# Splitting the softmax denominators of the last three batches over three engines, and moving the last pair's denominators ahead of its values

## What is computed

```
scores = einsum('bnhl,bkl->bhnk', CqWqk, C_kv) / sqrt(32)
attn = softmax(scores, axis=-1)
V_up = (C_kv @ Wv_u).reshape(b, nkv, H, HD)
out = einsum('bhnk,bkhd->bnhd', attn, V_up)
```

## Time and profile before

| | us |
|---|---|
| median of 3 runs | 678.75 (678.68 to 680.32) |
| the profiled execution | 681.57 |
| its span, first to last instruction | 679.6 |
| PE busy | 591.6 (87%) |
| POOL busy | 424.9 (63%) |
| DVE busy | 442.2 (65%) |
| ACT busy | 303.8 (45%) |

### The profile page before, as it was taken

How to read it: one execution, slowest core, us unless ns; L and a number is a source line. 1 busy time by engine, 2 the same in 40 slices (tenths; PEclk the granted TensorE clock), 3 DMA queues, 4 the chain that set the end, 5 groups by cost and what they waited for, 6 DMA issues and landing times.

```text
span 679.6 us, 12918 instructions
## 1 busy us (share of the span) xinstructions
PE 591.6 (87%) x3856; PEld 306.8 (45%) x3856; DVE 442.2 (65%) x717; ACT 303.8 (45%) x641; POOL 424.9 (63%) x394
## 2 busy tenths in 40 slices
PE   4863988699999999998999999999999899986965
PEld 4331644353544554464456354455446444433322
DVE  2711796378776887489658867588758966745451
ACT  1330144335644374346534564337444744563450
POOL 5002027558965886598776896488659877789300
PEclk9895889799999999999989999999999999997896
DMA  8567630353116510481018311661048101100000
GB/s 310 211 210 245 236 119 18 78 210 166 43 29 228 211 44 1 115 323 57 17 42 271 154 43 31 225 215 43 1 130 333 32 15 47 43 9 1 22 1 14
DMA packets 31410, 77.22 MB, mean 114 GB/s; under 512 B 11378, under 2 KB 25042, under 8 KB 28915
## 3 DMA queue, kind: packets, MB, share of 16 engines
q1 hardware_dynamic: 31186, 75.36, 33.1%
q10 hardware_dynamic: 160, 1.05, 0.4%
HBM read 58.66 MB, written 2.88 MB: 91 GB/s over the span
## 4 chain that ended last, share of the span: by engine, by line
PE 62%; DVE 12%; issue 7%; POOL 6%; ACT 5%; SPq 3%; DMA 3%; POOLq 0%; ACTq 0%; DVEq 0%
PE st_ps L649 11%; PE mx_ps L677 10%; PE pv_ps L664 9%; POOL acc L1096 5%; PE mi_ps L459 4%; PE mi_ps L466 4%; PE mi_ps L453 4%; PE mi_ps L512 4%; SPq L371 3%; PE mi_ps L631 2%; DVE mx_p L1020 2%; DVE sm L982 2%; PE mi_ps L537 2%; DMA b_eff<-acc 2%; PE mi_ps L635 2%
## 5 line engine op out<-in xcount | busy, mean ns | idle before, releaser
L1096 POOL TENSOR_TENSOR acc<-acc,p_ring 125x448 f32<-125x448 f32 x300 | 359.8, 1199 | 49.2 <-ACT p_ring L833 23.5
L1020 DVE TENSOR_REDUCE mx_p<-mx_ps 128x1 f32<-128x500 f32 x336 | 210.7, 669 | 101.7 <-PE mx_ps L677 100.6
L833 ACT ACTIVATE p_ring<-st_ps 125x448 f32<-125x448 f32 x384 | 189.7, 544 | 171.4 <-PE st_ps L649 164.4
L649 PE MATMUL st_ps<-q_st,c_st 98*125 98x448 f32 x384 | 155.3, 432 | 13.4 <-ACT p_ring L833 7.7
L677 PE MATMUL mx_ps<-c_st,q_st 96*128 96x500 f32 x336 | 139.4, 446 | 14.9 <-DMA q_st<-q_hl 11.2
L649 PEld LDWEIGHTS st_ps<-q_st,c_st 98*125 98x125 f32 x384 | 68.7, 191 | 117.1 <-ACT p_ring L833 88.2
L1104 POOL TENSOR_TENSOR rstd<-mv,eps_col 128x1 f32<-128x1 f32 x24 | 4.6, 192 | 153.2 <-DVE mv L894 153.2
L664 PE MATMUL pv_ps<-p_ring,c_nat 125*32 125x448 f32 x768 | 94.4, 564 | 1.0 <-ACT p_ring L833 0.9
L677 PEld LDWEIGHTS mx_ps<-c_st,q_st 96*128 96x128 f32 x336 | 63.2, 196 | 41.4 <-issue 20.6
L1096 POOL TENSOR_TENSOR acc<-p_ring 125x448 f32<-125x448 f32 x30 | 36.6, 1221 | 27.3 <-ACT p_ring L833 27.3
L466 PE MATMUL mi_ps<-ctx_sb,wkv_sb 128*32 128x375 f32 x512 | 48.1, 496 | 0.7 <-DVE p L943 0.7
(11 more groups left out here) (111 smaller groups left out, 671.0 us busy)
## 6 DMA issues: line engine op xcount, KB each, us to landing
ctx_sb<-in_ctx_t SPq DMA_DIRECT2D x16, 3000.0 KB, 11.1
c_st<-ct_hl SPq DMA_DIRECT2D x192, 46.9 KB, 2.0
q_st<-q_hl SPq DMA_DIRECT2D x96, 56.0 KB, 2.0
x_sb<-in_x SPq DMA_DIRECT2D x16, 112.0 KB
out_y<-x3n SPq DMA_DIRECT2D x16, 112.0 KB
wq_sb<-in_wq SPq DMA_DIRECT2D x2, 512.0 KB, 4.4
ctx_sb<-in_lora_a SPq DMA_DIRECT2D x1, 1024.0 KB, 6.8
ctx_sb<-in_lora_b SPq DMA_DIRECT2D x1, 1024.0 KB, 8.7
```

What stands on the lines that cost most here:

```text
L649: mm(st_ps[unit % STB][0:KC, 0:HALF], c_st[:, b % 4, t * KT + k * KC:t * KT + (k + 1) * KC], q_st[:, b // 2 % 2, b % 2, half * HALF:(half ...
L833: act.activation(p_ring[:, unit % PR, :], st_ps[unit % STB][0:KC, 0:HALF], ACT.Exp, scale=float(L) ** -0.5).then_inc(exp_done, 1)
L1020: ve.tensor_reduce(mx_p[:, p:p + 1], mx_ps[unit % MXB][:, 0:KP], AX.X, ALU.max).then_inc(red_done, 1)
L1096: po.tensor_tensor(dst, first, p_ring[:, unit % PR, :].rearrange("p (h s) -> p h s", s=S), ALU.add).then_inc(acc_done, 1)
```

## The change

Of the 32 halves POOL keeps 29. DVE adds up (13,1), (14,1) and (15,0), with a semaphore of its own (`acc_dve`), group by group, each group one step later and after the step's other work of DVE; before, it added both halves of batch 15. The denominators of (15,1) are not added elementwise: `last_counts` multiplies each of its units with ones on PE, 16 matmuls a group that accumulate in a bank of the maxima, ahead of the group's `sums`. For the last pair the order of the end is a list of its own (`LAST_STEPS`): DN and Y in step 7, DT in step 8, and DN and DT are in banks of the maxima. DN there multiplies only what was added (16 heads of batch 14, 8 of batch 15). ACT's copy to `den` leaves out the unused columns, which a new memset on POOL at the start fills with 1.0.

```diff
+LAST_STEPS = {6: ["XC"], 7: ["DN", "Y"], 8: ["DT"], 9: ["YT", "N2"], 10: ["T3"], 11: ["F1", "Fh", "F2"]}
+DVE_HALVES = [(B - 3, 1), (B - 2, 1), (B - 1, 0)]
+PE_HALF = (B - 1, 1)
+def pool_adds(b, half):
+    return ADDS * (b * 2 + half - sum(h < (b, half) for h in DVE_HALVES + [PE_HALF]))
+def dve_adds(b, half):
+    return ADDS * sum(h < (b, half) for h in DVE_HALVES)
...
         def step_bank(name, n):
+            if n == PAIRS - 1 and name in ("DN", "DT"):
+                return mx_ps[int(name == "DT")]
...
+                elif name == "DN" and n == PAIRS - 1:
+                    pe.wait_ge(acc_done, due(acc_done, pool_adds(B, 0)))
+                    pe.wait_ge(acc_dve, due(acc_dve, dve_adds(B, 0)))
+                    for b, heads in ((0, H), (1, H // 2)):
+                        for t in range(4):
+                            cells = o[t * L:(t + 1) * L, :].rearrange("p (q b s) -> p q b s", q=4, b=2)
+                            last = mm(cells[:, 0:heads // 4, b, 0:S], ones[0:KC, :],
+                                      acc[:, slot, t:heads:4, b * SLOT:b * SLOT + S], start=True, stop=True)
...
+            def last_counts(b, g):
+                half, k = g // KG, g % KG
+                pe.wait_ge(exp_done, due(exp_done, b * 24 + g * 4 + 4))
+                if k == 0:
+                    pe.wait_ge(red_done, due(red_done, B * PIECES))
+                for u in range(4):
+                    ring = p_ring[:, (b * 24 + g * 4 + u) % PR, :].rearrange("p (q t s) -> p t q s", q=2, t=4)
+                    for t in range(4):
+                        cells = mx_ps[0][t * L:(t + 1) * L, :].rearrange("p (q b s) -> p q b s", q=4, b=2)
+                        mm(cells[:, half * 2:half * 2 + 2, 1, 0:S], ones[0:KC, :], ring[:, t, :, :],
+                           start=(k == 0 and u == 0), stop=(k == KG - 1 and u == 3))
...
+                        if t == 1 and (bl, gl // KG) == PE_HALF:
+                            last_counts(bl, gl)
                         if t == 1 and 0 <= bl < B:
                             sums(bl, gl)
...
+                        added = (old // 24, old // 12 % 2)
+                        if added in DVE_HALVES:
+                            act.wait_ge(acc_dve, due(acc_dve, dve_adds(*added) + max(old % 12, 1)))
+                        elif added != PE_HALF:
+                            act.wait_ge(acc_done, due(acc_done, pool_adds(*added) + max(old % 12, 1)))
...
             def body(i):
-                if i == PAIRS:
-                    add_up_last()
                 for g in range(2 * GROUPS):
...
                     for name, n in steps_of(i, g):
                         step(name, n, i, g)
+                    bl, gl = (bm - 1, gg - 1) if gg else (bm - 2, GROUPS - 1)
+                    if (bl, gl // KG) in DVE_HALVES:
+                        add_up(bl, gl)
...
             def add_up(b, half, since=1, until=ADDS):
+                if (b, half) in DVE_HALVES:
+                    return
...
+            make(po.memset(den[:, :], 1.0))
```

More of the change, by code:

```diff
@@ L58 @@
 FIRST_LOOPED, LAST_LOOPED = 1, 6
-IDENT_MADE, MASKS_MADE, PADS_MADE, ALL_MADE = 2, 6, 10, 12
+IDENT_MADE, MASKS_MADE, PADS_MADE, ALL_MADE = 2, 6, 11, 13
 PIECES_IN = [3, 2, 4, 3, 0, 0, 0, 3, 4, 1, 3, 0]
@@ L103, in steps_of @@
 def steps_of(i, g):
+    if i == PAIRS:
+        for name in LAST_STEPS.get(g, []):
+            yield name, PAIRS - 1
+        return
     done = sum(PIECES_IN[g // GROUPS * GROUPS:g + 1])
@@ L253, in decoder_layer @@
         acc_done = sem("acc_done", 4 * ADDS)
+        acc_dve = sem("acc_dve", 0)
         mx_done = sem("mx_done", 2 * PIECES)
@@ L598, in step @@
                                   ox[:, h, :, :].rearrange("p b s -> p (b s)"), start=True, stop=True)
+                elif name == "DN" and n == PAIRS - 1:
[6 more added lines that the diff above has]
+                                      acc[:, slot, t:heads:4, b * SLOT:b * SLOT + S], start=True, stop=True)
                 elif name == "DN":
                     pe.wait_ge(yu_sb, due(yu_sb, n + 1))
-                    pe.wait_ge(acc_done, due(acc_done, 4 * ADDS * (n + 1)))
+                    pe.wait_ge(acc_done, due(acc_done, pool_adds(2 * n + 2, 0)))
+                    if n == PAIRS - 2:
+                        pe.wait_ge(acc_dve, due(acc_dve, dve_adds(2 * n + 2, 0)))
                     for t in range(4):
@@ L816, in step @@
                 elif name == "DN":
-                    copy(den[:, :], o[:, :]).then_inc(dn_sb, 1)
+                    copy(den[:, :].rearrange("p (q b s) -> p q b s", q=4, b=2)[:, :, :, 0:S],
+                         o[:, :].rearrange("p (q b s) -> p q b s", q=4, b=2)[:, :, :, 0:S]).then_inc(dn_sb, 1)
                 elif name == "T3":
@@ L831, in exponentials @@
                         act.wait_ge(pv_done, due(pv_done, old // 4 + 1))
-                        act.wait_ge(acc_done, due(acc_done, old // 12 * ADDS + max(old % 12, 1)))
+                        added = (old // 24, old // 12 % 2)
[3 more added lines that the diff above has]
+                            act.wait_ge(acc_done, due(acc_done, pool_adds(*added) + max(old % 12, 1)))
                     act.activation(p_ring[:, unit % PR, :], st_ps[unit % STB][0:KC, 0:HALF], ACT.Exp,
@@ L997, in softmax_end, with add_up @@
                     .then_inc(soft_n, 1)
-            def add_up_last():
-                b = B - 1
-                ve.wait_ge(acc_done, due(acc_done, 2 * b * ADDS))
-                for half in range(2):
-                    dst = acc[:, b // 2 % 2, half * 8:(half + 1) * 8, b % 2 * SLOT:b % 2 * SLOT + S]
-                    for k in range(1, ADDS + 1):
-                        unit = (b * 2 + half) * 12 + k
-                        ve.wait_ge(exp_done, due(exp_done, unit + 1))
-                        if k == 1:
-                            first = p_ring[:, (unit - 1) % PR, :].rearrange("p (h s) -> p h s", s=S)
-                        else:
-                            ve.wait_ge(acc_done, due(acc_done, (b * 2 + half) * ADDS + k - 1))
-                            first = dst
-                        ve.tensor_tensor(dst, first, p_ring[:, unit % PR, :].rearrange("p (h s) -> p h s", s=S),
-                                         ALU.add).then_inc(acc_done, 1)
+            def add_up(b, g):
+                half = g // KG
+                dst = acc[:, b // 2 % 2, half * 8:(half + 1) * 8, b % 2 * SLOT:b % 2 * SLOT + S]
+                for t in range(4):
+                    unit = b * 24 + g * 4 + t
+                    k = unit % 12
+                    if k == 0:
+                        continue
+                    ve.wait_ge(exp_done, due(exp_done, unit + 1))
+                    if k == 1:
+                        first = p_ring[:, (unit - 1) % PR, :].rearrange("p (h s) -> p h s", s=S)
+                    else:
+                        ve.wait_ge(acc_dve, due(acc_dve, dve_adds(b, half) + k - 1))
+                        first = dst
+                    ve.tensor_tensor(dst, first, p_ring[:, unit % PR, :].rearrange("p (h s) -> p h s", s=S),
+                                     ALU.add).then_inc(acc_dve, 1)
             def reduce_piece(b, p):
@@ L1081, in add_up @@
             def add_up(b, half, since=1, until=ADDS):
+                if (b, half) in DVE_HALVES:
+                    return
                 if 0 <= b < B:
-                    base = (b * 2 + half) * ADDS
+                    base = pool_adds(b, half)
                     dst = acc[:, b // 2 % 2, half * 8:(half + 1) * 8, b % 2 * SLOT:b % 2 * SLOT + S]
```

## The result

| | before | after |
|---|---|---|
| median, us | 680.2 (674.4 to 683.8, 20 runs) | 686.0 (677.3 to 693.7, 20 runs) |
| ratio to before, 95% interval | | 1.0058 (1.0031 to 1.0084) |
| profiled execution, us (span) | 681.57 (679.6) | 689.16 (687.3) |
| mean granted clock in it | 0.947 | 0.935 |
| POOL's adds | 330 | 308 |

The forecast was 678.4 us, with six chances in ten that no change could be told. By the ratio the kernel is 0.58% slower, 3.9 us; by the medians it is 5.9 us. The ratio leaves out executions over 1.5% above the fastest, which are six of the changed kernel's 20 (its profiled one among them) and none of the 20 of before, so the profile shows the loss at its long end.

The account below looks back on a forecast made before the run. POOL's adds were taken to hold up body 7 near its end, with a chain of waits after it. Body 7 -0.9, ones products and DVE's queue +3.0, order -2.4 gave -0.3 on 678.75: 678.4 us, range 674.4 to 680.9.

Parts of the forecast that it names:

- The order of the last pair: Last pair, ox to YT: DN runs while ACT copies ox and x3; 2.75 us instead of 5.11, gain 2.4.
- DVE's four adds beside POOL's: Body 7, last four adds of (13,1), from 603.4 us: partly held up by POOL's adds, the fourth done at 608.4.
- The stops of PE in steps 7 and 10: Body 7: PE stands still 2.6 us before Y and 1.9 us after YT, both for DVE's reductions.
- YT of pair 6: Body 7: YT starts at 621.5 us against 615.03 before, 6.5 us later.
- Y to YT: Body 7, from 610.85 us: 8.46 us at full clock plus 2.2 us for the lower clock.
- The cost of the ones products at full clock: Three groups of (15,1) on PE: 0.9 us each, 2.7 us, part of it falling into PE's pauses for DVE.
- the tail to the last sums: From F2's DVE add (T) through batch 15's six groups: ends at T + 21.15 us, 3.0 us more than before.
- The queue's waits: Batch 15: exponentials 0 to 19 wait in turn for DVE's queued adds, up to 0.7 us later than PE alone.
- E: Rival, batch 15: ones products don't overlap over the four quarters, +8.1 us, 686.5 us; 3%.
- from YT to the end of body 7: After pair 6's YT (y), LN3 free of POOL: ends at y + 15.6 us, 7.4 less; body 7 ends 0.9 us earlier.
- a second fall of the clock: In PE's 1.9 us stop after YT: T3 1.6 us later, all but 0.65 hidden by the wait for DVE's add.
- theory 1: Formed after the traces, tail: DVE's queue makes PE pause, the clock falls, and ones products keep PE from working it off.

Follow-up runs that it names:

- filled: The changed kernel with one unread score matmul more behind each score of groups 0 to 3 of batch 15: 1.0015 of before.
- queue_no_counts: The changed kernel without the ones products, DVE adding up (15,1) too: 1.0020 of before.
- pool131: The changed kernel with half (13,1) given back to POOL, DVE keeping (14,1) and (15,0): 0.9997 of before.
- filled_all: filled with 9 and 7 more unread matmuls at two stops of PE in body 7: 0.9956 of before.
- early_order: Against before: DVE adds (13,1), early in the step, and both halves of batch 15; no ones products; new order of the last pair: 0.9902.
- early_order_filled: early_order with unread matmuls in three pauses of PE, 8 each at two stops in body 7 and 18 behind the last YT: 0.9836 of before, median 667.8 us.

## Why the prediction was wrong

**What held.** The order of the last pair: 2.60 us from ox to YT, forecast 2.75, and 2.73 with it alone. DVE's four adds beside POOL's: 5.0 us forecast, 2.9 without POOL, 5.39 measured. The Trainium skill (SBUF — State Buffer, "Who interferes with whom") has the later instruction blocked for the whole of the earlier. By that rule the prediction had 5.9 us; the trace lies between 5.0 and 5.9, and agrees that DVE's adds are held up beside POOL's. The stops of PE in steps 7 and 10: forecast 2.6 and 1.9, measured 2.29 and 1.99. YT of pair 6: 621.5, measured 621.26, which is 0.4 us later than forecast when the earlier start of body 7 is taken off; the clock, though, fell not in the stop of 2.29 us but at about 605.7, right after that of 1.35. That Y to YT still took 10.6 us (forecast 10.66) is in part luck: PE mostly stood still in the 3 us by which the fall came early. The cost of the ones products at full clock: 2.7 less what DVE's pauses hide; measured 2.2 by themselves.

**What failed: the tail to the last sums.** The step followed six groups instruction by instruction, with eight adds queued behind F2, and came to T + 21.15. With the clock held up it is 22.1 (`filled`, with 16 matmuls more), so the order of the waits was right to a microsecond. But every duration in it was one at 2.4 GHz. The same text had asked, for a stop of PE in body 7, what it does to the clock, and it did not ask that of the tail, where PE paused four times in 4 us, for 0.68 us and three times for 0.26. In the profiled execution the clock fell at 643.2 and stayed low for 20.5 us; measured 28.7 us to the end of the last sums, 7.6 over the step's sum and 10.7 over before. The queue's waits were short too: put at 0.7 us in the step's bounds, they measure 1.4 by themselves (19.5 in `queue_no_counts`, 18.1 before). No rival had the low clock in the tail, E's three chances in a hundred for slow ones products included, which is why the range ended at 680.9.

**A smaller miss: from YT to the end of body 7.** Forecast y + 15.6, or 16.2 with a second fall of the clock; measured 17.0. The clock did fall in the 1.99 us stop, at 626.2, and was back only near 633, so that T3, sums and F1 ran at half speed; the wait for the first add of (14,1), which was to hide most of that, hid none of it: the add was done at 629.3, and PE, at half speed, came to its last scores only at 630.99. This case was named but not taken for the sum, although the text says itself that the stop is as long as the one that had let the clock fall before.

**The sum.** Body 7 +0.9 instead of -0.9, tail +10.7 instead of +3.0, order -2.5 instead of -2.4, the rest -0.7 instead of 0, and -0.7 from the earlier start of body 7: +7.7 in the profiled executions. By the ratio it is 3.9 us; that the tail's clock is not lost equally in all executions would explain the difference, but only one of them has a trace. The forecast also started from a median of 678.75 us over 3 executions, which over 20 is 680.2: 1.4 of the 7.6 us between forecast and measured median. Across the 20 of the changed kernel the time follows the mean granted clock closely (correlation -0.94): the fastest, 677.3 us, has 0.962, the slowest, 693.7 us, 0.931.

**What stays open.** The same four pauses behind DVE's queue were followed by the low clock in the traces of the changed kernel and of `pool131`, and not in that of `queue_no_counts`. What decides it, and why it lasted 20.5 us in the one and 6.8 in the other, isn't shown, as each kernel has one trace. That the ones products keep the clock from coming back, the last part of theory 1, isn't shown either: in `pool131` it was back before the first of them, in the changed kernel it had been low for 11.7 us by then. How much of body 7's differences is the kernels' own isn't shown either. That DVE beside POOL costs body 7 its microseconds rests on the 5.39 us for four adds here and the same 5.39 to 5.40 in five other kernels; no run had POOL idle there with all else equal.

## What to carry to other kernels

A part of the kernel that runs at another engine's pace has to be asked two things: how long the matrix engine pauses, and whether it still does enough to keep its clock. Here eight adds put behind a late instruction of DVE cost 1.4 us in waits and, in the traced executions, between nothing and 6.6 us in clock. Before work is moved to another engine, look at where in that engine's queue it will stand: the same adds at the start of the step instead of its end made 1.3% of the kernel, the clock's part in it included. Before a half goes back to an engine, look at who waits for its last add: the new order put DN ahead of Y, and where DVE was late, that cost up to 4 us. And where a pause can't be avoided, matmuls that nobody reads, short enough to end before the wait does, took `filled` from 1.0015 to 0.9956 (`filled_all`, the intervals lie apart) and `early_order` from 0.990 to 0.984 (`early_order_filled`, the intervals just overlap).

## What the runs showed of the hardware

In the changed kernel the granted clock fell at 643.2 us with no pause of PE over 0.7 us in the 4 us ahead of it (639 to 643 us, busy 2.5 of 4), and once at 1.2 GHz it stayed there for 20 us while PE was busy for 1.74 to 2.00 of every 2 us. In `queue_no_counts` it stayed at 2.4 GHz through the same pauses (633 to 637 us, busy 2.5 of 4). In body 7 it fell after stops of 1.3 to 2.3 us, but the time until it was back differed within one trace from 3.4 us (`filled`, 626.5 to 629.9) to 10.2 (`filled`, 606.0 to 616.2). At 1.2 GHz the eight matmuls of a group's sums took 1.72 us, at 2.4 GHz 0.96.

A DVE addition of 125x448 with two SBUF inputs took 0.63 us alone, and four took 5.39 us beside POOL's adds.
